# Dispatched rows of two expert stages read already turned, by transposing DMAs, in place of turns on TensorE

## The chip, the cores and the metric

The kernel runs on one core of one Trainium2 chip. The metric is the device time of one execution in microseconds (us); less is better. The time before is the median of three runs, 3177.68 us (3175.09 to 3180.09).

## The reference, cut to what matters

The input `x` is 16 x 256 = 4096 tokens of 256 features. Eight layers follow one another: four attention-like layers (`xattn`) and four feed-forward layers (`ffn`), each added to `x`. The change lies in two of the feed-forward layers, both mixtures of experts:

```python
# layer 0: each expert takes up to 512 tokens of each of the two choices
scores = softmax(xf @ router_w); weights, experts = top_k(scores, 2)
for k in range(2):
    xe = xf[tokens of expert e, at most 512]
    y  = gelu(xe @ w1[e]) @ w2[e]           # 256 -> 1024 -> 256
    out += y * weights[:, k]
...
# layer 1: no capacity; eight experts, two for each token, and one shared expert
g, u = x @ w_gate[e], x @ w_up[e]           # 256 -> 352
eo   = (silu(g) * u) @ w_down[e]            # 352 -> 256
```

## The kernel before

The kernel is written as stages, one after the other, each with its own queues for the five engines (`nc.Block`) and semaphores between them. Ahead of an expert stage a router decides the row of every token, and tokens are scattered by indirect DMAs into a table `rows` in memory, sorted by expert. A row of the table has 512 half-precision numbers: 256 high parts of a token's features and 256 low parts, so 1 KB. The value is kept as a sum of the two, and products are made of three terms (high x high, low x high, high x low).

`experts_stage` (line 1233) computes the experts. It is called four times; the argument `raw` (the table `rows`) is given in two of these calls, and only those are touched:

- **l0e** (line 2871): 8 experts, each with two blocks of 512 rows, so 16 blocks (`gt` = 4 tiles of 128 rows, `gn` = 512). The weights are loaded in single precision by SyncE's queue and split by ScalarE and VectorE (`convert`).
- **l1e** (line 2899): 39 blocks of 256 rows (`gt` = 2, `gn` = 256). The weights of a block come already split from `packed`, by one indirect DMA of GpSimd's queue for each block, 4 blocks ahead.

The work is a list `plan` of units. For each pair of blocks (`a` = 0 and 1) the units are: up of block 0, up of block 1, down of block 0, down of block 1. An up unit multiplies the weights (the matmul's stationary side) by the turned rows `xT` (features on the partitions, rows along the free side) into the PSUM tile `H`: 8 chunks of 6 matmuls of 512 columns in l0e, 3 chunks of 2 x 6 matmuls of 256 columns in l1e (line 1529). ScalarE applies the activation into `hf` (1586); VectorE multiplies by the gate in l1e (1619) and splits into `hh` (1625) and `hl` (1627). A down unit multiplies `hh` and `hl` by the second weights into `Y` (1544), 24 matmuls of 256 columns for a tile of 128 rows in l0e and 9 in l1e. VectorE copies `Y` to `y` (1635), and SyncE stores `y` to `results` (1400).

For a matmul the rows must be turned, with the features on the partitions. Before the change this takes three steps:

- SyncE loads a block as it lies into `rb` (line 1408), a ring of 4 (l0e) or 6 (l1e) buffers; it waits for `turned` before a buffer is taken again.
- TensorE turns it, in `turn(b)` (line 1486): for each half of 256 rows 8 transposes of 128 x 128 into the PSUM tile `T`. Blocks 0 and 1 are turned ahead of the first unit, and later ones after the second up unit of a pair and after its first down unit (`next_block`).
- ScalarE copies `T` to `xT` (line 1568), in `copy(b)`, one instruction for each half of 256 rows; `xT` has two buffers.

An up unit waits for `copied`. The order on each queue is written out by hand: SyncE's in l0e for expert n is the rows of block 2n, the weights of expert n, the rows of block 2n + 1, the stores of expert n - 1; in l1e six row loads at the start, then for each block its store and one row load. GpSimd copies an identity matrix at the start of both stages (line 1443).

Because `T` takes PSUM, `Y` has two banks with two tiles in each, and a tile of a down unit waits until VectorE has copied the tile two before it (`DEPTH` = 2).

## Time and profile before

| | |
|---|---|
| median of 3 runs | 3177.68 us (3175.09 to 3180.09) |
| span of the profiled execution, first to last instruction | 3092.9 us |
| what lies around the span (median less span) | 84.8 us |
| TensorE busy (matmuls) | 2527.4 us, 82% of the span |
| VectorE busy | 2162.5 us, 70% |
| ScalarE busy | 1301.5 us, 42% |
| GpSimd busy | 1035.7 us, 33% |
| DMA | 266.65 MB, mean 86 GB/s |
| l0e, first row load to last copy of a result | 494.5 to 854.8 us |
| l1e, first row load to last matmul of a down unit | 1155.3 to about 1415 us |

The profile is of one execution; of that execution the profile gives the span and no time of its own, so the median of the runs stands beside it. Times within it are counted from its first instruction. "PE" is TensorE, "PEld" its weight loads, "DVE" VectorE, "ACT" ScalarE, "POOL" GpSimd and "SPq" SyncE's queue. A matmul's duration in a row (some 270 ns for 256 columns) is that of one alone; they overlap, so what a series costs is read from the distance of the starts.

### The profile page before, as it was taken

The page shows a single profiled execution, that of the slowest core. Times are in us where ns is not written, and L with a number is a line of the kernel's source. Part 1 is how long each engine was busy: PE and PEld are TensorE (multiplying, and loading weights), DVE is VectorE, ACT ScalarE, POOL GpSimd, SP SyncE. Part 2 cuts the span into 40 slices and gives each one's busy share as a digit, 9 for nine tenths or more (in the row PEclk, how much of TensorE's full clock was granted, in tenths as well). Part 3 has the DMA queues.
Part 4 walks back from the last instruction along what each step waited for, and adds up shares of the span by engine and source line. Part 5 has one row for each costly group of instructions (what it writes and reads, how often), then busy time and mean ns, then how long its engine had stood idle before and what let it go on. Part 6 is the DMA issues. An engine that isn't in the chain of part 4 may idle for free. (4 is left out here: it accounts for less than half of the span.)

```text
span 3092.9 us, 57450 instructions
## 1 busy us (share of the span) xinstructions
PE 2527.4 (82%) x21340; PEld 1655.3 (54%) x21340; DVE 2162.5 (70%) x5536; ACT 1301.5 (42%) x2296; POOL 1035.7 (33%) x1446
## 2 busy tenths in 40 slices
PE   1989386999915599997999778885899999979973
PEld 0443264677614358995466544444565555656662
DVE  5898764665567766665678688977766555867757
ACT  1777443433312223332366646772322222356622
POOL 3452272110065361114466387861300000034330
PEclk9999588999957699998999888997999999979996
DMA  3331173332140247775611031100200000011001
GB/s 98 124 123 71 62 267 135 110 110 71 60 153 21 81 169 276 259 254 182 201 59 43 17 125 43 44 12 3 65 21 1 1 1 1 6 42 49 22 10 60
DMA packets 158280, 266.65 MB, mean 86 GB/s; under 512 B 23003, under 2 KB 106249, under 8 KB 151988
## 3 DMA queue, kind: packets, MB, share of 16 engines
q1 hardware_dynamic: 131316, 186.70, 18.1%
q0 software_dynamic: 17904, 76.23, 7.2%
q8 instruction: 172, 2.82, 0.4%
q10 hardware_dynamic: 8784, 0.04, 0.2%
q14 instruction: 104, 0.85, 0.1%
HBM read 174.99 MB, written 88.34 MB: 85 GB/s over the span
## 5 line engine op out<-in xcount | busy, mean ns | idle before, releaser
L1586 ACT ACTIVATE l2e_hf<-l2e_H 128x512 f32<-128x512 f32 x208 | 124.2, 597 | 381.9 <-PE l2e_H L1529 381.9
L1718 POOL TENSOR_TENSOR all_m_rstd<-all_m_sq,all_mhalf 128x8 f32<-128x8 f32 x24 | 39.6, 1649 | 558.4 <-DVE all_m_sq L1703 524.0
L788 DVE TENSOR_REDUCE l0a_mx<-l0a_S 128x2 f16<-128x512 f32 x256 | 167.8, 686 | 20.1 <-PE l0a_S L622 19.4
L1625 DVE CAST l2e_hh<-l2e_hf 128x512 f16<-128x512 f32 x208 | 92.8, 446 | 122.9 <-ACT l2e_hf L1586 108.6
L1529 PE MATMUL l0e_H<-l0e_xT,l0e_w 128*128 128x512 f16 x768 | 168.1, 381 | 0.0
L737 ACT ACTIVATE l0a_pf<-l0a_ST 128x512 f32<-128x512 f32 x256 | 146.6, 602 | 51.1 <-PE l0a_ST L636 50.9
L784 DVE CUSTOM_DVE_ANT_0 l2s_masked<-l2s_S,l2s_mq 128x128 f32<-128x128 f32 (+1 forms) x512 | 153.1, 349 | 19.5 <-PE l2s_S L622 19.3
L1529 PE MATMUL l2e_H<-l2o_hi,l2e_w 128*128 128x512 f16 x576 | 151.7, 382 | 15.8 <-DVE l2e_w L1601 15.8
L1529 PE MATMUL l1e_H<-l1e_xT,l1e_w 128*128 128x256 f16 (+1 forms) x1404 | 158.7, 275 | 2.8 <-DMA l1e_w<-packed,all_second_weight_row 2.8
L1529 PE MATMUL l2e_H<-l2e_hh,l2e_w 128*128 128x512 f16 x640 | 155.1, 379 | 0.0
L1627 DVE TENSOR_TENSOR l2e_hl<-l2e_hf,l2e_hh 128x512 f16<-128x512 f32 x208 | 147.2, 708 | 7.2
L1529 PEld LDWEIGHTS l1e_H<-l1e_xT,l1e_w 128*128 128x128 f16 (+1 forms) x1404 | 143.7, 107 | 15.3 <-DMA l1e_w<-packed,all_second_weight_row 3.1
L737 ACT ACTIVATE l2s_pf<-l2s_ST 128x384 f32<-128x384 f32 x256 | 119.3, 496 | 53.6 <-PE l2s_ST L636 53.1
L1586 ACT ACTIVATE l0e_hf<-l0e_H 128x512 f32<-128x512 f32 x128 | 76.4, 597 | 141.2 <-PE l0e_H L1529 141.2
L2689 POOL DMA_INDIRECT l1n_yb<-results,all_first_read x64 | 62.5, 977 | 196.0 <-POOLq L57 176.8
L1544 PE MATMUL l0e_Y<-l0e_w,l0e_hh 128*128 128x256 f16 x1024 | 124.7, 273 | 0.0
L1529 PEld LDWEIGHTS l0e_H<-l0e_xT,l0e_w 128*128 128x128 f16 x768 | 75.4, 98 | 89.7 <-issue 1.4
L788 DVE TENSOR_REDUCE l3a_mx<-l3a_S 128x2 f16<-128x512 f32 x128 | 88.2, 693 | 41.1 <-PE l3a_S L622 39.8
L581 POOL TENSOR_SCALAR_AFFINE_SELECT l2s_pf<-l2s_pf 128x256 f32<-128x256 f32 x256 | 100.9, 406 | 46.5 <-ACT l2s_pf L737 46.4
L1544 PE MATMUL l2e_Y<-l2e_w,l2e_hh 128*128 128x192 f16 x1024 | 109.5, 248 | 3.7 <-DVE all_x L1641 3.7
L788 DVE TENSOR_REDUCE l2a_mx<-l2a_S 128x2 f16<-128x512 f32 x128 | 87.5, 690 | 30.0 <-PE l2a_S L622 29.1
L1544 PEld LDWEIGHTS l0e_Y<-l0e_w,l0e_hh 128*128 128x128 f16 x1024 | 99.5, 98 | 11.6
(706 smaller groups left out, 7258.5 us busy)
## 6 DMA issues: line engine op xcount, KB each, us to landing
l0e_wf<-in_L_ffn_w SPq DMA_DIRECT2D x16, 1024.0 KB, 8.8
rows<-l0a_zeros SPq DMA_DIRECT2D x16, 640.0 KB, 5.9
l1e_rb<-rows SPq DMA_DIRECT2D x39, 256.0 KB, 9.0
results<-l1e_y SPq DMA_DIRECT2D x39, 256.0 KB, 2.2
l0a_kv<-in_ctx SPq DMA_DIRECT2D x16, 512.0 KB, 4.1
rows<-l0a_zeros SPq DMA_DIRECT2D x16, 512.0 KB, 4.9
l0d_p_cx<-in_ctx SPq DMA_DIRECT2D x16, 512.0 KB, 6.4
l0e_rb<-rows SPq DMA_DIRECT2D x16, 512.0 KB, 9.6
```

What stands on the lines that cost most here:

```text
L581: nc.gpsimd.affine_select(out=t, in_=t, compare_op=ALU.is_ge, fill=0.0, base=0, pattern=[[0, TB], [1, P]], channel_multiplier=-1).then_inc ...
L737: nc.scalar.activation(pf[n % NPF][:, 0:used], ST_ps[n % 2][:, 0:used], ACT.Exp).then_inc(probs, 1)
L784: m = nc.vector.tensor_tensor_reduce(masked[n % 2][u][:, 0:key_to[u]], ps[:, s_at[u]:s_at[u] + key_to[u]], mq[:, S - key_to[u]:S], 1.0, -3 ...
L788: m = nc.vector.tensor_reduce(mx[h % 2][:, :, i], ps[:, :].rearrange("p (u k) -> p u k", u=TB), AX.X, ALU.max)
L1529: mm = pe.matmul(bank[0:fn, :], W[par][0:kn, at + k * wd + f0:at + k * wd + f0 + fn], X, start=(done == 0), stop=(done == k_all - 1))
L1544: mm = pe.matmul(Y[u][:, 0:wd], X[0:kn, k, u * P:u * P + P], W[par][0:kn, at + k * wd:at + (k + 1) * wd], start=(done == 0), stop=(done == ...
L1586: nc.scalar.activation(hf[q % 4][0:fn, :], pair_of(q, lay)[0][0:fn, :], lay.func, scale=1.0 / WS).then_inc(acted, 1)
L1625: nc.vector.tensor_copy(high, v).then_inc(hi_done, 1)
L1627: nc.vector.tensor_tensor(low, v, high, ALU.subtract).then_inc(split, 1)
L1718: self.nc.gpsimd.tensor_tensor(out=(self.rstd, self.rstd2)[which][:, g], in0=(self.sq, self.sq2)[which][:, g], in1=self.g.mhalf[:, 0:self. ...
L2689: nc.gpsimd.indirect_dma_start(yb[n % NB][:, :], None, rows[:, :], bass.IndirectOffsetOnAxis(ap=to.read_row[n % 2][:, n // 2:n // 2 + 1], ...
```

## The change

The rows of a block are read by one DMA with a transpose (`dma_start_transpose`) straight from the table into `xT`, which now has the ring's depth (4 buffers in l0e, 6 in l1e). The tiles `rb`, `T` and `ident_h`, the functions `turn` and `copy`, the semaphores `turned` and `copied` and GpSimd's copy of the identity are gone. An up unit waits for `rows_in` of its block. SyncE waits with a buffer's next load for `upped` at the number of chunks that ends the up unit of the block that held it (`read_by`). `Y` has `gt` banks of its own, and a down tile waits for the copy of the tile `gt` before it.

```diff
--- before.py
+++ after.py
@@ -1242,13 +1242,12 @@
     tiles = 2 * gt * NPAIR if packed is None else gt
     NE = len(experts)
     STG = max(-(-a // P) * b for e in experts for a, b in e.mats)
-    HALVES, BLKS = gt // 2, NE * tiles // gt
+    BLKS = NE * tiles // gt
     RING = 4 if packed is None else 6
-    DEPTH = gt if raw is None else 2
     NW = min(2 if packed is None else 4, NE)
     cols = [max(e.cols for e in experts[i::NW]) for i in range(NW)]
 
-    plan, bank_of, bank_free, reads_of = [], [], [], {}
+    plan, bank_of, bank_free, reads_of, read_by = [], [], [], {}, []
     chunk = tile = bank = 0
     last_in = [None] * 4
     for first in range(0, NE, 1 if packed is None else 2):
@@ -1277,6 +1276,8 @@
                                 last_in[b] = chunk
                             chunk += 1
                         split_to[(l, a)] = chunk
+                        if l == 0:
+                            read_by.append(chunk)
                         if l:
                             reads_of[(a, (l - 1) % n_hbuf)] = ("upped", chunk)
                     else:
@@ -1316,17 +1317,10 @@
         hl = [[st.sb(f"hl{a}{i}", [P, FT, gn], F16) for i in range(n_hbuf)] for a in range(2)]
         hf = [st.sb(f"hf{i}", [P, gn]) for i in range(4)]
         H = st.ps("H", [P, 4, 512])
-        if raw is None:
-            Y = [st.ps(f"Y{i}") for i in range(gt)]
-        else:
-            pairs = [st.ps(f"Y{i}") for i in range(2)]
-            Y = [pairs[u % 2][:, u // 2 * D:(u // 2 + 1) * D] for u in range(gt)]
-            T = [st.ps(f"T{i}", [P, 2, KD, 2, P], F16) for i in range(2)]
-            rb = [st.sb(f"rb{i}", [P, gt, 2 * D], F16) for i in range(RING)]
-            xT = [st.sb(f"xT{i}", [P, 2, KD, gn], F16) for i in range(2)]
-            ident_h = st.sb("ident_h", [P, P], F16)
+        Y = [st.ps(f"Y{i}") for i in range(gt)]
+        if raw is not None:
+            xT = [st.sb(f"xT{i}", [P, 2, KD, gn], F16) for i in range(RING)]
             rows_in = [st.sem(f"rows_in{i}") for i in range(RING)]
-            ident_set, turned, copied = st.sem("ident_set"), st.sem("turned"), st.sem("copied")
 
         w_in = [st.sem(f"w_in{i}") for i in range(NSTG)]
         w_hi, w_lo = st.sem("w_hi"), st.sem("w_lo")
@@ -1404,10 +1398,9 @@
                     if raw is None or b >= BLKS:
                         return
                     if b >= RING:
-                        sp.wait_ge(turned, (b - RING + 1) * HALVES)
-                    sp.dma_start(rb[b % RING][:, :, :],
-                                 raw[b * gn:(b + 1) * gn, :].rearrange("(t p) d -> p t d", p=P)
-                                 ).then_inc(rows_in[b % RING], 16)
+                        sp.wait_ge(upped, read_by[b - RING])
+                    sp.dma_start_transpose(xT[b % RING][:, :, :, :].rearrange("p r k q -> p (r k) q"),
+                                           raw[b * gn:(b + 1) * gn, :]).then_inc(rows_in[b % RING], 16)
 
                 for n in range(NE):
                     if packed is None:
@@ -1439,8 +1432,6 @@
 
             @block.gpsimd
             def _(pool):
-                if raw is not None:
-                    nc.gpsimd.tensor_copy(ident_h[:, :], g.ident[:, :]).then_inc(ident_set, 1)
                 if pack is not None:
                     pack.fill(nc)
                 if send is not None:
@@ -1463,35 +1454,8 @@
                         w_all[n % NW][:, :], None, packed[:, :],
                         bass.IndirectOffsetOnAxis(ap=c[:, n:n + 1], axis=0)).then_inc(w_got[n % NW], 16)
 
-            def next_block(un):
-
-                if raw is None or (un.l, un.a) not in ((0, 1), (1, 0)):
-                    return BLKS
-                first = 2 * un.n if packed is None else un.n // 2 * 2
-                return first + (2 if un.l == 0 else 3)
-
             @block.tensor
             def _(pe):
-                def turn(b):
-                    if raw is None or b >= BLKS:
-                        return
-                    pe.wait_ge(rows_in[b % RING], (b // RING + 1) * 16)
-                    for j in range(HALVES):
-                        h = b * HALVES + j
-                        if h >= 2:
-                            pe.wait_ge(copied, h - 1)
-                        for r in range(2):
-                            for k in range(KD):
-                                for u in range(2):
-                                    m = pe.transpose(T[h % 2][:, r, k, u, :],
-                                                     rb[b % RING][:, 2 * j + u, r * D + k * P:r * D + (k + 1) * P],
-                                                     ident_h[:, :])
-                        m.then_inc(turned, 1)
-
-                if raw is not None:
-                    pe.wait_ge(ident_set, 1)
-                turn(0)
-                turn(1)
                 for un in plan:
                     ex, par, a = experts[un.n], un.n % NW, un.a
                     lay, m0 = layer_of(un), first_of_layer(ex, un.l)
@@ -1507,7 +1471,7 @@
                         col = (un.i * 2 + a) * gn if packed is None else 0
                         if raw is not None:
                             b = 2 * un.n + a if packed is None else un.n
-                            pe.wait_ge(copied, (b + 1) * HALVES)
+                            pe.wait_ge(rows_in[b % RING], (b // RING + 1) * 16)
                         for f, (f0, fn) in enumerate(lay.chunks):
                             q = un.at + f
                             before = bank_free[q]
@@ -1523,7 +1487,7 @@
                                         if un.l:
                                             X = (hh if x_hi else hl)[a][(un.l - 1) % n_hbuf][0:kn, k, :]
                                         elif raw is not None:
-                                            X = xT[a][:, 0 if x_hi else 1, k, :]
+                                            X = xT[b % RING][:, 0 if x_hi else 1, k, :]
                                         else:
                                             X = (hi if x_hi else lo)[:, k, col:col + gn]
                                         mm = pe.matmul(bank[0:fn, :],
@@ -1535,8 +1499,8 @@
                         at, wd = place(ex, m0), ex.mats[-1][1]
                         for u in range(gt):
                             t = un.at + u
-                            if t >= DEPTH:
-                                pe.wait_ge(added, t - DEPTH + 1)
+                            if t >= gt:
+                                pe.wait_ge(added, t - gt + 1)
                             k_all, done = 3 * len(lay.kt), 0
                             for W, x_hi in ((wh, True), (wh, False), (wl, True)):
                                 for k, (k0, kn) in enumerate(lay.kt):
@@ -1546,7 +1510,6 @@
                                                    start=(done == 0), stop=(done == k_all - 1))
                                     done += 1
                             mm.then_inc(downed, 1)
-                    turn(next_block(un))
 
             @block.scalar
             def _(act):
@@ -1559,20 +1522,8 @@
                                          wf[p.slot][0:p.rows, p.src:p.src + p.cols], ACT.Copy, scale=WS
                                          ).then_inc(w_hi, 1)
 
-                def copy(b):
-                    if raw is None or b >= BLKS:
-                        return
-                    for j in range(HALVES):
-                        h = b * HALVES + j
-                        act.wait_ge(turned, h + 1)
-                        nc.scalar.activation(xT[b % 2][:, :, :, j * 2 * P:(j + 1) * 2 * P],
-                                             T[h % 2][:, :, :, :, :].rearrange("p r k u q -> p r k (u q)"), ACT.Copy
-                                             ).then_inc(copied, 1)
-
-                copy(0)
                 for k in of_expert[0]:
                     convert(k)
-                copy(1)
                 if send is not None:
                     send.hi_parts(nc, act)
                 for un in plan:
@@ -1591,7 +1542,6 @@
                                 convert(later[t])
                         if pack is not None and un.a == 0:
                             pack.hi_part(act, un.i)
-                    copy(next_block(un))
 
             @block.vector
             def _(dve):
```

**TensorE in l1e, the first pair of blocks and the next.** `H` is the up units, `T` the turns, `Y` the down units. Before:

```order
L1529 MATMUL l1e_H<-l1e_xT,l1e_w 128x256 x24
L1529 MATMUL l1e_H<-l1e_xT,l1e_w 96x256 x12
L1529 MATMUL l1e_H<-l1e_xT,l1e_w 128x256 x24
L1529 MATMUL l1e_H<-l1e_xT,l1e_w 96x256 x12
L1486 MATMUL l1e_T<-l1e_ident_h,l1e_rb 128x128 x8
L1544 MATMUL l1e_Y<-l1e_w,l1e_hh 128x256 x3
L1544 MATMUL l1e_Y<-l1e_w,l1e_hl 128x256 x3
L1544 MATMUL l1e_Y<-l1e_w,l1e_hh 128x256 x6
L1544 MATMUL l1e_Y<-l1e_w,l1e_hl 128x256 x3
L1544 MATMUL l1e_Y<-l1e_w,l1e_hh 128x256 x3
L1486 MATMUL l1e_T<-l1e_ident_h,l1e_rb 128x128 x8
L1544 MATMUL l1e_Y<-l1e_w,l1e_hh 128x256 x3
```

With the change:

```order
L1493 MATMUL l1e_H<-l1e_xT,l1e_w 128x256 x24
L1493 MATMUL l1e_H<-l1e_xT,l1e_w 96x256 x12
L1493 MATMUL l1e_H<-l1e_xT,l1e_w 128x256 x24
L1493 MATMUL l1e_H<-l1e_xT,l1e_w 96x256 x12
L1508 MATMUL l1e_Y<-l1e_w,l1e_hh 128x256 x3
L1508 MATMUL l1e_Y<-l1e_w,l1e_hl 128x256 x3
L1508 MATMUL l1e_Y<-l1e_w,l1e_hh 128x256 x6
L1508 MATMUL l1e_Y<-l1e_w,l1e_hl 128x256 x3
L1508 MATMUL l1e_Y<-l1e_w,l1e_hh 128x256 x6
L1508 MATMUL l1e_Y<-l1e_w,l1e_hl 128x256 x3
```

The groups of 8 transposes between the up and the down units and between the two down units are gone; nothing else changes its place. In l0e it is the same with groups of 16.

**SyncE's queue in l0e, from expert 2 on.** `results` is the store, `wf` the weights; the brackets name the semaphore that is waited for. Before:

```order
L1408 DMA l0e_rb<-rows 128x4x512 [waits l0e_turned]
L1389 DMA l0e_wf<-in_L_ffn_w 128x2x1024 [waits l0e_w_lo]
L1389 DMA l0e_wf<-in_L_ffn_w 128x8x256 [waits l0e_w_lo]
L1408 DMA l0e_rb<-rows 128x4x512 [waits l0e_turned]
L1400 DMA results<-l0e_y 128x4x256 [waits l0e_added] x2
```

With the change:

```order
L1402 DMA_TRANSPOSE l0e_xT<-rows 128x4x512 [waits l0e_upped]
L1383 DMA l0e_wf<-in_L_ffn_w 128x2x1024 [waits l0e_w_lo]
L1383 DMA l0e_wf<-in_L_ffn_w 128x8x256 [waits l0e_w_lo]
L1402 DMA_TRANSPOSE l0e_xT<-rows 128x4x512 [waits l0e_upped]
L1394 DMA results<-l0e_y 128x4x256 [waits l0e_added] x2
```

The row loads keep their places in the queue and become transposes; their wait is for `upped` (TensorE's up unit) in place of `turned`.

## Rows read from the trace of the kernel before

**Rows 1.** the page: busy time of each engine, and the granted TensorE clock over 40 slices
```profile
PE 2527.4 (82%) x21340; PEld 1655.3 (54%) x21340; DVE 2162.5 (70%) x5536; ACT 1301.5 (42%) x2296; POOL 1035.7 (33%) x1446
...
PEclk9999588999957699998999888997999999979996
```

**Rows 2.** windows: a stretch of l0e and one of l1e (busy us, instructions, clock, DMA share, GB/s)
```profile
540.00:820.00 280.00, 280.00 (x2072) 193.66 (x2070) 174.47 (x307) 111.76 (x179) 21.05 (x29) 1.00 0.29 95
1180.00:1400.00 220.00, 220.00 (x2143) 202.22 (x2142) 146.24 (x382) 74.91 (x139) 30.92 (x33) 1.00 0.74 259
```

**Rows 3.** TensorE's waits in 505:856 (first row), its groups in 1155:1420 (the others)
```profile
PE l0e_T L1486 <- DMA l0e_rb<-rows: 5.2, 1, 5.2
...
L1529 PE MATMUL l1e_H<-l1e_xT,l1e_w 128*128 128x256 f16 (+1 forms) x1404 | 158.7, 275 | 2.8 <-DMA l1e_w<-packed,all_second_weight_row 2.8
L1544 PE MATMUL l1e_Y<-l1e_w,l1e_hh 128*128 128x256 f16 (+1 forms) x468 | 70.4, 272 | 1.7 <-DVE l1e_hl L1627 1.7
L1486 PE MATMUL l1e_T<-l1e_ident_h,l1e_rb 128*128 128x128 f16 x312 | 24.4, 224 | 6.9 <-DMA l1e_rb<-rows 6.9
```

**Rows 4.** tiles T of both stages: count, duration ns min/median/max, first and last start
```profile
L1486 PE MATMUL l0e_T<-l0e_ident_h,l0e_rb x256: 218/219/315, 498.4 to 802.0; 128*128 128x128 f16 x128
L1568 ACT ACTIVATE l0e_xT<-l0e_T x32: 1018/1021/1032, 499.5 to 802.7; 128x1024 f16<-128x1024 f16 x32
...
L1486 PE MATMUL l1e_T<-l1e_ident_h,l1e_rb x312: 217/219/315, 1158.9 to 1403.2; 128*128 128x128 f16 x156
```

**Rows 5.** timeline of TensorE in l0e: turns of one block (start us, us, engine ...)
```profile
615.88 1.06 PE L1486 MATMUL l0e_T<-l0e_ident_h,l0e_rb 128*128 128x128 f16 x16
616.77 1.04 PE L1544 MATMUL l0e_Y<-l0e_w,l0e_hh 128*128 128x256 f16 x8
```

**Rows 6.** timeline of l1e, one pair of blocks: TensorE and VectorE
```profile
1203.97 8.02 PE L1529 MATMUL l1e_H<-l1e_xT,l1e_w 128*128 128x256 f16 x72
...
1211.83 0.61 PE L1486 MATMUL l1e_T<-l1e_ident_h,l1e_rb 128*128 128x128 f16 x8
...
1212.28 0.49 PE L1544 MATMUL l1e_Y<-l1e_w,l1e_hh 128*128 128x256 f16 x3
...
1213.22 0.42 DVE L1627 TENSOR_TENSOR l1e_hl<-l1e_hf,l1e_hh 96x256 f16<-96x256 f32 x1
...
1213.56 0.41 DVE L1635 COPY l1e_y<-l1e_Y 128x256 f32<-128x256 f32 x1
...
1214.27 0.61 PE L1486 MATMUL l1e_T<-l1e_ident_h,l1e_rb 128*128 128x128 f16 x8
...
1214.71 0.49 PE L1544 MATMUL l1e_Y<-l1e_w,l1e_hh 128*128 128x256 f16 x3
...
1216.70 0.49 PE L1529 MATMUL l1e_H<-l1e_xT,l1e_w 128*128 128x256 f16 x3
```

**Rows 7.** timeline of the start of l0e
```profile
494.47 0.36 SPq L1408 DMA_DIRECT2D l0e_rb<-rows  x1
...
501.95 2.50 DVE L1601 SCALAR_TENSOR_TENSOR l0e_w<-l0e_wf,l0e_w 128x512 f16<-128x512 f32 x4 [29.45 <-ACT l0e_w L1558]
...
505.48 1.89 PE L1486 MATMUL l0e_T<-l0e_ident_h,l0e_rb 128*128 128x128 f16 x16 [5.19 <-DMA l0e_rb<-rows]
...
507.16 18.07 PE L1529 MATMUL l0e_H<-l0e_xT,l0e_w 128*128 128x512 f16 x78
```

**Rows 8.** DMA in 1180:1400 (queue: packets, MB, share of 16 engines; issue: KB, us to landing)
```profile
q0 software_dynamic: 5015, 38.78, 48.8%
q1 hardware_dynamic: 18485, 17.82, 24.8%
...
l1e_rb<-rows SPq DMA_DIRECT2D x32, 256.0 KB, 9.0
```

**Rows 9.** the page's queue of the smallest packets; SP's issue times of the l1e rows, ns
```profile
q10 hardware_dynamic: 8784, 0.04, 0.2%
...
L1408 SPq DMA_DIRECT2D l1e_rb<-rows x39: 371/473/1306, 1155.3 to 1380.9; - x39
```

## The prediction

> **What bounds the kernel now.** I read the page first. Over the span TensorE is the busiest engine with 82%, but that is an average over stages with different limits [rows 1]; what the change is worth must be read in the two stages that it touches. The second view is the windows of their steady parts [rows 2]. In 280 us of l0e and in 220 us of l1e TensorE's matmuls fill every microsecond, at a granted clock of 1.00 (2.4 GHz), while VectorE is busy 62% and 66%, ScalarE 40% and 34%. The third view is TensorE's waits [rows 3]: in the whole of l0e from 505 us on it waits once, 5.2 us at the start, for the rows of block 1; in l1e three times, for rows 6.9, for weights 2.8 and for a low half 1.7 us, all in the first pair of blocks. So TensorE's own time sets both stages, and what is taken from its queue comes off the span, as long as nothing else becomes later than TensorE. DMA engines are the next candidate: they are used 0.29 in l0e but 0.74 in l1e [rows 2].
>
> **What is removed.** There are 256 and 312 transposes [rows 4]. Their duration (218 ns) is not their price, since they overlap; the price is the distance from the first of a group to the next instruction. In l0e the 16 of a block take 616.77 - 615.88 = 0.89 us [rows 5]; in l1e the 8 of a block 1212.28 - 1211.83 = 0.45 and 1214.71 - 1214.27 = 0.44 us [rows 6].
>
> - l0e, blocks 2 to 15: 14 x 0.89 = 12.5 us off the path.
> - l1e, blocks 2 to 38: 37 x 0.445 = 16.5 us off the path. Blocks 0 and 1 are turned while TensorE waits for the first weights anyway [rows 3], so they give nothing.
> - Start of l0e: the first up unit begins at 507.16, behind the turns of block 1, which begin at 505.48, when its rows land. The first weight matrix is split at 501.95 + 2.50 = 504.45 [rows 7]. With the change the unit needs only that and block 0, whose transfer is issued at 494.47, 10 us earlier; block 1 is not needed until the unit after it. The gain is at most 507.16 - 504.45 = 2.7 us, and nothing if block 0's slower transfer holds up the weights behind it. I take 2.
> - ScalarE's copies (32 of 1.02 us in l0e, 39 in l1e) [rows 4] lie beside TensorE's work, which never waits for them. They give nothing. GpSimd's copy of the identity, 0.3 us, lets the first weight gather of l1e start earlier, but six transposes stand beside it: nothing. The two more banks of Y in l0e remove a wait that TensorE does not show; in l1e the depth stays 2.
>
> **What is late next.** In l1e the down unit of block 1 of a pair needs the last low half of its up unit, and its first tile needs the copy of the first tile of the unit before (depth 2). Before, the last up matmul is followed by 0.45 of turns, 1.99 of the first down unit and 0.44 of turns. The low half is done at 1213.22 + 0.42 = 1213.64 and the copy, which VectorE takes right behind it, at 1213.56 + 0.41 = 1213.97; TensorE comes at 1214.71 [rows 6]. Without the turns it comes at 1211.83 + 1.99 = 1213.82, ahead of the copy. VectorE's chain hangs on the up unit's end and does not move. So there is a new wait of 0.15 us, and about 0.1 to 0.2 more for the release and for filling the pipeline again, which is not shown before; I take 0.3, from 0 to 0.6. Over 19 pairs that gives back 5.7 us (0 to 11.4). In l0e the first down unit of a pair is 10.5 us long (four tiles of 24 matmuls), so nothing of this arises there.
>
> **What is added: 16 transposes of 512 KB and 39 of 256 KB.** No row shows one. First the time at which they are asked for: SyncE's new wait is for the up unit of the block 4 or 6 earlier, which stands behind a store that waited for that block or a later one, so it never decides, and the stores behind it are not held. A block of l1e is read about five blocks (30 us) ahead of its use, a landing now takes 9.0 us [rows 8], so what matters is throughput, not latency.
>
> The price of throughput: in l1e the DMA engines work 0.74 x 220 us; a pair takes 1216.70 - 1203.97 = 12.73 us [rows 6], a block 6.37, so 4.71 us of DMA for each block. The hardware queue has 24.8% of 220 us = 54.6 us for 34.5 blocks, half rows and half stores (both 256 packets of 1 KB): 0.79 us for the 256 rows, and 3.92 us for all the rest [rows 8]. The new period by TensorE is 6.37 - 0.445 + 0.15 = 6.07 us. **TensorE stays the bound if a transpose of 256 rows costs at most 6.07 - 3.92 = 2.15 us of DMA, 2.7 times the plain transfer.** In l0e there is far more room (0.29 of 21.7 us).
>
> The bounds. Below: 0.79 us, the plain transfer; a quicker one would gain nothing, as TensorE does not wait for these transfers past the start. Above: two adjoining numbers of a row go to two partitions. If each became a packet of its own, at the 0.2% x 16 x 3092.9 / 8784 = 11 ns of the page's smallest packets [rows 9], a block would cost 131072 x 11 ns / 16 = 90 us, and the kernel over 3 ms more. In between, the nearest row is the landing of the same rows, 9.0 us, were one transpose to hold its queue that long. I take under 2.15 us, since the same number of bytes and the same kind of queue are nearest to the plain row; this is my least certain choice. Issuing takes SyncE 0.37 to 1.3 us for the plain load [rows 9], one instruction for each block as before; it has 6 us for each.
>
> By the rows, a 128 x 128 turn on TensorE is worth 0.056 us of its time. The Trainium skill ("VectorE: DVE Perf Modes", The three transpose paths) gives 1309 ns for one through the DMA crossbar; eight of them one after another would be an estimate of 10.5 us for a block of l1e. The same skill ("Advanced Engine Details and Errata", X-Bar Transpose (TRN2)) holds that transposing DMAs are as fast as ordinary ones, which would leave the sum as it stands. No row of before can decide between them.
>
> **The sum.** 12.5 + 2 + 16.5 - 5.7 = 25.3 us less. The span was 3092.9, so 3067.6; the median of the runs is 84.8 above the span, which I leave as it is: 3177.7 - 25.3 = **3152 us**, 0.8% faster. Its own range, by the start (0 to 2.7) and the new wait (0 to 11.4): 3144 to 3160.
>
> **The rivals.**
>
> 1. Transposes that don't fit beside l1e's other traffic (the other side). Place: the DMA engines or SyncE's queue in l1e. Mechanism: a transposing transfer costs several times its bytes, or they run one at a time. From 2.15 us for a block it shows; from 2.45 l1e loses what it gained; from about 2.8 (2.45 + 14.5 / 39), 3.6 times the plain price, the kernel is slower. Priced by the landing row, 9.0 us for each block: (9.0 - 6.37) x 39 = 103 more in l1e, 14.5 less in l0e, where 21.7 us still hold it: 3266 us. For it: l1e's engines have only a quarter to spare, small packets cost far more for a byte, and the turned layout is made of small pieces. Against it: l0e hides anything up to some 16 us, and a queue with 30 us of lead evens out bursts. Chance 0.35. By the skill's 1309 ns for a tile, 10.5 us, it would be (10.5 - 6.37) x 39 - 14.5, or 3324.
> 2. Half of it: transposes of about 3 times the plain price. l1e is where it was, l0e keeps its 14.5: 3163, between 3160 and 3180. Chance 0.17.
> 3. The new wait is not there, because VectorE's chain moves with TensorE's, or a release is quicker: 3146. It lies within the forecast's own range and has no chance of its own.
>
> **How the numbers follow.** Forecast 0.48, rival 1 0.35, rival 2 0.17. A measurement of this kernel can tell about 0.2%, 6.4 us, from no change, so "same" is 3171 to 3184. Faster: 0.48 and 0.11 of rival 2, 0.59; same: the other 0.06 of it; slower: 0.35. The range begins at 3142, just under the forecast's own. To leave no more than 2 in 10 out it must reach through rival 2 and half of rival 1, to 3270.
>
> **What would show it.** Right: no L1486 rows; in the windows a pair of l1e at about 12.1 us and an expert of l0e at 41.7 in place of 43.5; TensorE still without waits in l0e and, in l1e, 19 waits of 0.2 to 0.4 us for VectorE's copy or low half; the first up unit of l0e at about 505. The transposes' landing within 20 us, and the DMA share of l1e under 0.9. Wrong: waits of TensorE for DMA into xT or w in l1e (rival 1 or 2, by their sum), SyncE's issues of several microseconds, or stores that land so late that VectorE waits for `stored`.

## The result, and the profile after

The changed kernel takes 3198.22 us (median of 20 runs, 3179.18 to 3235.61), the kernel before beside it 3180.03 us (20 runs, 3173.57 to 3185.43). The ratio is **1.0068 [1.0049, 1.0088]: slower by 0.7%**, where 0.8% faster was forecast. The range of 3142 to 3270 holds it, but only because it was drawn wide enough for the rivals; the forecast's own 3144 to 3160 misses it. The ratios here and below are of the fast runs alone, which leaves out any run more than 1.5% above the fastest of its kernel (here one of the 20). The spread is news too: 56 us from the fastest to the slowest run, against 12 for the kernel before.

The windows of the kernel after, in the order l0e (the stretch of [rows 2]), then l1e, its columns as in [rows 2]:

```profile
540.00:820.00 280.00, 280.00 (x1911) 186.74 (x1909) 185.40 (x327) 91.78 (x160) 20.29 (x28) 1.00 0.37 94
...
1260.00:1280.00 20.00, 19.86 (x182) 18.03 (x181) 14.29 (x38) 4.58 (x12) 2.42 (x3) 1.00 1.13 235
1280.00:1320.00 40.00, 30.07 (x245) 25.63 (x244) 18.45 (x50) 4.58 (x12) 4.68 (x5) 0.87 1.04 206
1320.00:1360.00 40.00, 39.58 (x359) 35.50 (x357) 26.98 (x71) 7.64 (x20) 6.55 (x7) 1.00 1.07 270
```

l0e is as clean as before, and l1e is not: in one stretch of 40 us TensorE is busy 30, its clock is 0.87, and the DMA engines, though over 1.0 busy, move 206 GB/s where the next stretch moves 270.

**l0e** went nearly as forecast. The answer to [rows 7] and [rows 3], from the timeline of its start (TensorE), and the last down units from the tile's listing (count, duration, first and last start):

```profile
504.20 8.17 PE L1493 MATMUL l0e_H<-l0e_xT,l0e_w 128*128 128x512 f16 x26 [24.59 <-DVE l0e_w L1551]
```

```profile
L1508 PE MATMUL l0e_Y<-l0e_w,l0e_hh x1024: 272/273/273, 527.3 to 839.9; 128*128 128x256 f16 x171
```

In the trace of before the same listing ends at 854.1, 14.2 us later, where 14.5 were forecast. But 1.3 of these are an earlier begin of the whole stage in this execution: its first row load is issued at 493.18, that of before at 494.47. From this load to the last down matmul l0e takes 359.6 us before and 346.7 after, so 12.9 us were won (13.6 in e1, 13.5 in e13). The turns' 12.5 are there: an expert takes 631.63 - 589.95 = 41.68 us, 43.46 before. The start gave 0.4 here (1.1 in e1): the first up unit begins 1.7 us sooner after the first load, but 1.3 are lost again in its first matmuls. They now run while the granted clock is still 0.50 (windows 504:506 and 506:508; 1.00 from 510 on), a time that before was mostly spent on the turns. TensorE waits for nothing else in the stage.

**l1e** took 1501.2 - 1229.4 = 271.8 us from its first up to its last down matmul; before it was 1414.9 - 1163.6 = 251.3. The answer to [rows 6], a pair of blocks where nothing disturbs it (timeline, TensorE):

```profile
1259.17 8.02 PE L1493 MATMUL l1e_H<-l1e_xT,l1e_w 128*128 128x256 f16 x72
1267.03 0.49 PE L1508 MATMUL l1e_Y<-l1e_w,l1e_hh 128*128 128x256 f16 x3
...
1268.69 1.12 PE L1508 MATMUL l1e_Y<-l1e_w,l1e_hh 128*128 128x256 f16 x6
...
1269.98 0.82 PE L1508 MATMUL l1e_Y<-l1e_w,l1e_hh 128*128 128x256 f16 x6
...
1271.31 4.86 PE L1493 MATMUL l1e_H<-l1e_xT,l1e_w 128*128 128x256 f16 x43
```

A pair takes 1271.31 - 1259.17 = 12.14 us; 12.1 was forecast. The new wait is in it too: the six matmuls across the border of the down units take 1.12 where six others take 0.82, so 0.30. If all pairs were like this one, the forecast would have held. (TensorE's matmuls show no wait here; its weight loads do, 17 times, 8.3 us in all, for VectorE's low half `hl` and not for its copy.) The losses stand in the chain of waits of l1e (engine, what waits, for what: us, times, longest):

```profile
DVE l1e_y L1585 <- DMA results<-l1e_y: 36.2, 13, 15.0
...
PE l1e_H L1493 <- DMA l1e_xT<-rows: 13.8, 1, 13.8
...
PE l1e_H L1493 <- DMA l1e_w<-packed,all_second_weight_row: 12.6, 2, 11.0
...
PE l1e_H L1493 <- DVE l1e_hf L1569: 7.3, 1, 7.3
...
PE l1e_Y L1508 <- DVE l1e_y L1585: 2.7, 2, 1.8
```

The first wait for weights (11.0) is the stage's start and is nothing new: from the last matmul of l1s to the first up matmul pass 11.3 us, before 11.9. New are 13.8 us for the rows of block 1, then 7.3 + 2.7 + 1.6 for things that hang on VectorE and on a late gather, and the lower clock behind such pauses. VectorE in turn waits 36 us for its stores. Why the stores are late is seen in SyncE's queue (timeline; the duration is that of issuing), the answer to [rows 9]:

```profile
1221.69 29.68 SPq L1402 DMA_TRANSPOSE l1e_xT<-rows  x6
...
1273.43 17.04 SPq L1402 DMA_TRANSPOSE l1e_xT<-rows  x1
1290.52 3.45 SPq L1394 DMA_DIRECT2D results<-l1e_y  x1
...
1307.10 1.27 SPq L1402 DMA_TRANSPOSE l1e_xT<-rows  x1
...
1309.13 5.21 SPq L1402 DMA_TRANSPOSE l1e_xT<-rows  x1
```

Merely to issue a transpose holds SyncE 1.3 us at best, 5.2 in the second of two that follow one another within 2.3 us, and here 17.04. The store behind that one leaves at 1290.52. VectorE gets its buffer back at 1297.44 and TensorE, behind it, resumes at 1298.67:

```profile
1297.44 0.76 DVE L1585 COPY l1e_y<-l1e_Y 128x256 f32<-128x256 f32 x2 [15.03 <-DMA results<-l1e_y]
```

The plain loads of before took 0.47 us in the median [rows 9]. The answer to [rows 8], in a stretch without a jam (a jam is a time in which the DMA engines are busy, move little and TensorE pauses; 1306 to 1366; queue: packets, MB, share of 16 engines; q1 is SyncE's, q0 the weight gathers):

```profile
q0 software_dynamic: 1438, 11.13, 54.6%
q1 hardware_dynamic: 12813, 5.13, 49.0%
```

Packets are now of 256 bytes for the rows, 1024 for a block where there were 256.

Two facts about the times are needed below. Chips differ: the kernel before takes about 3178 us beside e1 to e4 and 3094 beside e5 to e15, so times are compared only with before of the same chip, as a ratio or a difference. And most of the difference is one stage that the change doesn't touch, l1s, which takes 170.6 us from its first to its last matmul in the kernel after and 103.0 in the profile of before. The kernel after, l1s, TensorE's waits:

```profile
PE l1s_Y L1508 <- issue: 58.5, 23, 12.9
```

e1 to e4 show 56 to 59 us of it, e5 to e15 none. The changed kernel shows it in e1 and not in e13, so the change does not bring it. The profile of before, like that of e8, has none, which is most of its 84.8 us between span and median. The expected times of e5 to e7 were still written for a kernel before of 3178 us; they are read as differences to it.

### The profile page after: what moved, and what is told of

The parts are those of the page before. It is cut to its first block and busy times, and to the rows that moved or that the text cites. A ratio compares the mean times of both kernels' runs of the same rounds, so it can differ in the third digit from the quotient of the medians.

```text
span 3184.9 us, 56187 instructions
## 1 busy us (share of the span) xinstructions
PE 2507.9 (79%) x20772; PEld 1618.7 (51%) x20772; DVE 2160.3 (68%) x5536; ACT 1231.4 (39%) x2225; POOL 1028.7 (32%) x1444
## 5 line engine op out<-in xcount | busy, mean ns | idle before, releaser
L1493 PE MATMUL l1e_H<-l1e_xT,l1e_w 128*128 128x256 f16 (+1 forms) x1404 | 163.4, 279 | 33.7 <-DMA l1e_xT<-rows 13.8
L1493 PE MATMUL l2e_H<-l2o_hi,l2e_w 128*128 128x512 f16 x576 | 151.5, 381 | 15.8 <-DVE l2e_w L1551 15.8
L1537 ACT ACTIVATE l1e_hf<-l1e_H 128x256 f32<-128x256 f32 (+1 forms) x117 | 44.7, 382 | 240.4 <-PE l1e_H L1493 200.6
L1453 POOL DMA_INDIRECT l1e_w<-packed,all_second_weight_row x39 | 36.6, 939 | 308.0 <-PE l1e_Y L1508 220.5
```

Of the source, the lines that this page charges most:

```text
L1453: nc.gpsimd.indirect_dma_start(w_all[n % NW][:, :], None, packed[:, :], bass.IndirectOffsetOnAxis(ap=c[:, n:n + 1], axis=0)).then_inc(w_go ...
L1493: mm = pe.matmul(bank[0:fn, :], W[par][0:kn, at + k * wd + f0:at + k * wd + f0 + fn], X, start=(done == 0), stop=(done == k_all - 1))
L1537: nc.scalar.activation(hf[q % 4][0:fn, :], pair_of(q, lay)[0][0:fn, :], lay.func, scale=1.0 / WS).then_inc(acted, 1)
```

## The experiments

In a name, l0 and l1 are the stages l0e and l1e.

**e1_again: the changed kernel, unaltered.**

> The changed kernel unchanged, for a second profile. Theory A (the transposes of l1e overload the DMA engines: a 256-byte packet of a transpose takes about 35 ns against 12 for as many bytes of a plain one): 3185 to 3215 us; l1e again with DMA share about 1.0 and waits of TensorE for xT, for weights and for stores in bursts; the stage l1s between the two transposing stages, where the first profile shows TensorE stuttering with 'issue' for 43 us, shows no stutter, as nothing is transposed there. Theory B (transposes disturb the fetching of instructions in later stages): the 43 us of 'issue' in l1s come again.

Measured: 3194.21 us against 3178.39, ratio 1.0063 [1.0047, 1.0080]; l1e 266.5 us, with the same waits (rows 13.5, weights 13.1, `hf` 5.2) and 32.9 us for the first six issues. The loss repeats, and so do the issue waits of l1s.

**e2_l0_only and e3_l1_only: the change in one stage alone.** The code of both ways, chosen by a flag:

```diff
-                  bias=..., raw=rows)
+                  bias=..., raw=rows, xbar=True)      # e2: call of l0e; e3: call of l1e
```

> Only l0e reads its rows by transposing DMAs; l1e turns on TensorE as before. Theory A: 14.2 us less than before (12.5 of turns, 1.7 of start), 3163 to 3168, runs close together as before. Theory B: the gain is eaten in l1s or elsewhere, 3178 or more, with a wide spread.

> Only l1e reads its rows by transposing DMAs. Theory A: before + 18 + 14 = about 3212 (3200 to 3230), with the wide spread of the changed kernel; l1s without 'issue'. Theory B, where the damage is done by l0e's transposes to stages behind them: at most 3180.

Measured: e2 3168.58 us, 0.9970 [0.9958, 0.9982], 9.8 us won; l1e stays at 250.7 us. Of the 12.9 us by which l0e is shorter in e2's trace too, 9.8 reach the medians; where the rest goes isn't shown. e3 3224.00 us, 1.0135 [1.0116, 1.0155], 45.6 us lost; l1e takes 298 us. So l0e gains most of what was forecast, and all of the loss is l1e's. e3's waits:

```profile
DVE l1e_y L1650 <- DMA results<-l1e_y: 67.6, 11, 17.6
...
PE l1e_H L1544 <- DVE l1e_hf L1634: 20.3, 3, 9.5
...
PE l1e_H L1544 <- DMA l1e_w<-packed,all_second_weight_row: 16.3, 2, 10.2
```

**e4_plain: the same bytes by plain DMAs.**

```diff
-sp.dma_start_transpose(xT[b % RING]..., raw[b * gn:(b + 1) * gn, :])
+sp.dma_start(xT[b % RING]..., raw[b * gn:(b + 1) * gn, :].rearrange("(t p) d -> p t d", p=P))
```

> The changed kernel with plain DMAs of the same bytes (1 KB packets) in place of the transposes; the rows are not turned, so the two expert stages compute with data in the wrong places, at the same shapes. It shows what the turns on TensorE alone are worth. Both theories: 3150 to 3156, as in my sum (14.2 in l0e, 10 to 14 in l1e), pairs of l1e of 12.1 us without hiccups, spread as narrow as before. If it is not faster than before, the loss has nothing to do with transposing.

Measured: 3155.55 us, 0.9925 [0.9913, 0.9938], 22.8 us won, where the forecast's sum was 25.3. l1e takes 239.5 us, 11.8 less than before (forecast 16.5 - 5.7 = 10.8). TensorE's waits in it are two, for the first weights and the first low half:

```profile
PE l1e_H L1495 <- DMA l1e_w<-packed,all_second_weight_row: 12.3, 1, 12.3
PE l1e_Y L1510 <- DVE l1e_hl L1579: 1.7, 1, 1.7
```

Its window 1300:1360 and SyncE's row loads in it (count, issue ns min/median/max):

```profile
1300.00:1360.00 60.00, 59.29 (x536) 53.11 (x534) 41.58 (x110) 11.45 (x30) 9.37 (x10) 1.00 0.78 271
```

```profile
L1402 SPq DMA_DIRECT2D l1e_xT<-rows x39: 370/472/1864, 1223.8 to 1439.2; - x39
```

So the terms on TensorE and VectorE hold, as a sum, to 2.5 us. What fails is what the transposing transfers do, and nothing else in the change.

**e5_pieces: plain DMAs in packets of 256 bytes.**

```diff
+for t in range(gt):
+    sp.dma_start(xT[b % RING][:, :, :, t * P:(t + 1) * P]...,
+                 raw[b * gn + t * P:...].rearrange("p (j q) -> p j q", q=P)).then_inc(rows_in[b % RING], 16)
```

> The changed kernel with plain DMAs that move the same bytes in as many packets as the transposes have (256 bytes each; one DMA for each 128 rows, so 2 and 4 for a block), rows not turned, so data in the wrong places. In the steady part of l1e the transposes cost 34 ns a packet, 2.2 us a block, against 48 ns for 1 KB. Theory A1 (it is the small packets): as slow a packet here, 30 to 35 ns, DMA share of l1e about 1.0, the time as the changed kernel's, about 3195. Theory A2 (it is the turning itself, which needs more than a small plain packet): a plain packet of 256 bytes takes 15 to 20 ns, share 0.8 to 0.85, time 3152 to 3160, as with plain packets of 1 KB.

Measured: 3073.56 us against 3093.87, 0.9934 [0.9921, 0.9948]; l1e 243.5 us, with a wait for rows of 3.2. Its queues in 1230:1290:

```profile
q0 software_dynamic: 1440, 11.14, 52.5%
q1 hardware_dynamic: 13205, 5.17, 32.2%
```

As many packets as in the kernel after, but q1 uses 32.2% and not 49.0%, and nothing jams. (These DMAs are two for a block, the transposes one.) So behind the start it is not the small packets but the turning that costs.

At the start the size of the packets does count. There are the queues of the kernel after in 1231:1246, while TensorE waits for the rows of block 1, and those of e5 in 1153:1159:

```profile
q0 software_dynamic: 346, 2.72, 67.6%
q1 hardware_dynamic: 837, 0.21, 33.9%
```

```profile
q0 software_dynamic: 304, 2.37, 95.7%
q1 hardware_dynamic: 305, 0.08, 5.7%
```

Beside the gathers (q0) the rows barely move in either, 14 and 13 GB/s. In e5 the two queues get as many packets each, and one of the rows' is 256 bytes; with packets of 1 KB (e4, 1234:1240) 308 beside 285 carry 48 GB/s. But in e5 the gathers run at 395 GB/s and are soon done, so TensorE waits 3.2 us for the rows; beside transposes they run at 181. When they are done in the kernel after, the rows move at 223 GB/s (1249:1252).

**e6_l0_twice and e7_l1_twice: each transpose a second time, into a spare buffer.**

```diff
+if twice:
+    sp.dma_start_transpose(spare[b % RING]..., raw[b * gn:(b + 1) * gn, :]).then_inc(spare_in[b % RING], 16)
```

> Only l0e transposes, and each of its 16 transposes is issued a second time, into a buffer that nobody reads. Theory A: l0e has room, with one transpose of 512 KB at 4.4 us of DMA and 4.7 of all the rest in 20.8 us a second one is hidden: the time of e2, 3165 to 3175 (weights land 4 us later but are split 10 us after landing). Rival: what counts is SyncE's time (2.3 to 8.5 us an issue) or the order behind it: then TensorE waits for weights at each expert, 3180 or more.

> Both stages transpose, and each of l1e's 39 transposes is issued a second time into a spare buffer. Theory A (DMA engines are full): a block of l1e then takes 3.9 + 2 x 2.2 = 8.3 us at the least against 6.07, so 39 x 2.2 = 87 us and more on the changed kernel: 3280 to 3330. Rival (hiccups come from order and start only, with time to spare on the engines): under 3230.

Measured: e6 3084.13 us, 0.9967 [0.9955, 0.9979], which is e2's ratio: in l0e even the second transpose is hidden, except at the start, where the first up unit comes 14.8 us behind the first load in place of e2's 11.1. e7 has four runs, 3161, 3167, 3236 and 3249 us, so 68 to 155 more than before (median 108), where 102 to 152 were expected by the theory of full engines and under 52 by its rival: neither holds as it stands. In its trace (of the 3167) l1e takes 336 us, 56 more than e13's, the DMA share 1.11 over 1180:1480 at 222 GB/s. The dose counts in l1e (the edit also makes SyncE wait for the spare buffer's load before) and not in l0e, where in 540:820 the share with two transposes is 0.48.

**e8_before_again: the kernel before, unaltered.**

> The kernel before, unchanged, for a second profile. Its first profile has a span 85 us under the time of its runs and no 'issue' waits of TensorE in l1s, while all five later profiles have about 57 us of them there, whatever is transposed, and spans within 15 us of their runs. If these waits belong to every execution and the first profile was the exception, this one shows them too, with a span of about 3165 to 3185; if they come from the changes, they are absent again.

Measured: 3095.71 us, span 3094.0, no issue waits in l1s. With e13 this says that they go with the chip, or the time at which it was used, and not with the change; it cleared most of the 84.8 us.

**e9_act_stores: l1e's stores go out from ScalarE's queue.**

```diff
+if packed is not None:
+    act.wait_ge(added, un.at + gt)
+    act.dma_start(rows_out[...], y[un.a][:, :, :]).then_inc(stored[un.a], 16)
```

> The changed kernel, but l1e's 39 stores are issued from ScalarE's queue, so that they no longer stand behind transposes whose issue takes up to 17 us on SyncE's queue. In the changed kernel VectorE waits 36 us in l1e for stores, and TensorE 7 to 10 us behind it. Theory A2 (DMA engines are full, 1.04 in the steady part, so every hiccup stays): the time stays near 1.006 of before, 1.002 at best. Theory C (the order in SyncE's queue makes the hiccups; the engines would keep up): 10 to 15 us less than the changed kernel, 1.001 to 1.003 of before.

Measured: 3084.77 us (3079.43 to 3086.04) against 3093.51, 0.9967 [0.9954, 0.9980]. TensorE's waits in l1e, all at its start:

```profile
PE l1e_H L1495 <- DMA l1e_w<-packed,all_second_weight_row: 10.4, 1, 10.4
...
PE l1e_H L1495 <- DMA l1e_xT<-rows: 9.9, 1, 9.9
...
PE l1e_Y L1510 <- DVE l1e_hl L1583: 1.7, 1, 1.7
```

Its window 1240:1300, and the queues in it (q1 now has transposes alone, q10 the stores):

```profile
1240.00:1300.00 60.00, 59.30 (x537) 53.08 (x535) 42.16 (x110) 11.48 (x30) 8.67 (x11) 1.00 1.00 274
```

```profile
q1 hardware_dynamic: 10560, 2.62, 33.5%
q10 hardware_dynamic: 2720, 2.62, 12.9%
```

The DMA share is 1.00 and TensorE runs as fast as in e4. "The engines are full" is therefore not what costs time. VectorE no longer waits for stores, the later pauses are gone, and the spread of the runs shrinks from 22 us (e13) to 7. Against the changed kernel 26 us were won (below), where 10 to 15 were expected. Two things changed, though. The stores no longer stand behind transposes; and the transposes no longer stand behind stores, so they leave 3.9 and 8.2 us apart, where the kernel after has 2.3 and 9.8, and issuing one is quick: 1.33 us in the median, and none over 2.1 once the first six are out (17.04 in the kernel after). So it is shown that stores and transposes in one queue cost the time behind the start. How much of it is stores that are held, and how much the transposes' own long issues, no run separates.

**e10_gate and e11_both: block 1's rows ahead of the third weight gather**; e11 has e9's stores as well.

```diff
+if n == 2:
+    pool.wait_ge(rows_in[1], 16)
```

> The changed kernel, but GpSimd issues l1e's third weight gather only when block 1's rows have landed. At the start of l1e six transposes and four gathers of 1.1 MB compete, and TensorE waits 13.8 us for block 1's rows. A transpose takes 5.2 us of SyncE's queue beside a gather and 1.3 us alone. If gathers slow the transposes, the 13.8 us fall to under 3 and the time by about 10 us: 1.003 of before. If the transposes are as slow by themselves, nothing is won.

> Both of the last two edits. If both are right: 0.997 to 1.000 of before, with l1e at about 245 us; still not the 0.9925 of plain packets, since the DMA engines are full.

Measured: e10 3110.26 us, 1.0050 [1.0027, 1.0073]; e11 3112.94, 1.0053 [1.0022, 1.0085]. The wait for rows fell from 13.8 to 5.7 us in e10, as meant, but weights then cost TensorE 24.5 us in four waits, and the time is that of the changed kernel (e13). e11 was expected at 0.997 to 1.000 with l1e at 245 us; l1e took 278, so the gate turned e9's 0.9967 into 1.0053. In e11, with the stores out of SyncE's queue, the windows of the start and of the time behind it are:

```profile
1180.00:1200.00 20.00, 11.44 (x76) 8.81 (x75) 4.32 (x12) 1.15 (x3) 1.07 (x2) 0.68 1.20 160
1200.00:1240.00 40.00, 29.80 (x225) 24.84 (x224) 17.04 (x46) 4.25 (x12) 4.41 (x5) 0.83 1.19 179
...
1300.00:1380.00 80.00, 79.16 (x716) 71.12 (x715) 55.82 (x147) 15.66 (x41) 12.07 (x13) 1.00 0.96 278
```

The engines are 1.2 busy and move 160 GB/s; 100 us later they move 278 at 0.96. Queue order is not all: there is a jam in the DMA itself. Stores in a queue of their own are late in it too (VectorE waits 30.8 us for them), and so are gathers (23.0 us of TensorE's waits, the 11.3 at the stage's start among them); TensorE's clock falls with such pauses (0.68).

**e12_mix: in l1e only the odd blocks come turned, the even ones as before.** l0e as in the change.

```diff
+dma_turned = lambda b: xbar or (half and b % 2 == 1)
```

> l0e transposes by DMA, in l1e only the odd blocks do, the even ones are turned on TensorE as before. Theory A2: DMA share of l1e in between, about 0.9, so no hiccups; TensorE is rid of 19 turns of 0.445 us, 8.5 us, on top of what l0e gives (0.997): 0.994 to 0.996 of before, the best of all correct kernels. Rival: even so a transpose beside a gather blocks SyncE's queue at times, and stores come late: 0.998 or more.

Measured: 3076.62 us (3070.97 to 3081.69), 0.9949 [0.9935, 0.9962], faster than both kernels, as expected. l1e 243.2 us, VectorE's waits for stores 3.5 us, no pause behind the start.

**e13_after_here, e14_flight, e15_mix_act: on one chip.** e13 is the changed kernel; e14 lets at most two transposes of l1e be in flight; e15 is e12 with e9's stores.

```diff
+if packed is not None and b >= 2:                      # e14
+    sp.wait_ge(rows_in[(b - 2) % RING], ((b - 2) // RING + 1) * 16)
```

> The changed kernel, unaltered, beside the two that follow, so that all are read against the same runs of before. On a chip where before takes 3094 us and shows no issue waits in l1s, every theory has before's time less 14.5 (l0e) plus what l1e loses, 15 to 21 us by the two traces of it so far: 3094 to 3101 us, ratio 1.000 to 1.002. If l1e's loss here is under 8 us, the loss itself depended on the chip; if the ratio stays at 1.006, something beside l1e is lost.

> The changed kernel, but in l1e SyncE starts a block's transpose only when the one two blocks ahead has landed, so at most two are in flight. If the jams come from several transposes that pile up (six at the start, and those that follow a pause) and SyncE's issues of 10 to 17 us are its queue's descriptors being full, no issue is over 6 us, TensorE's hiccups for hf, y and w behind the start go, and the time is 3070 to 3080 us. If the hold is a single transpose that meets a weight gather, issues of over 10 us stay, and with them the stores behind; time as that of the changed kernel or up to 10 us more, since SyncE now also waits.

> The mixed kernel (l0e turned by DMA; in l1e odd blocks by DMA and even ones on TensorE) with l1e's stores issued from ScalarE's queue. If what the transposes still cost the mixed kernel is stores held behind them in SyncE's queue, some of its waits at the start go and it takes 3070 to 3075 us. If at half the number no store is held (VectorE waited 3.5 us for stores there, TensorE not at all behind the start), it stays within 3 us of 3076.6, or gets up to 5 us slower by ScalarE's issues and waits ahead of its activations.

Measured, against 3094.29 of before: e13 3111.22 us, 1.0069 [1.0046, 1.0091], the ratio of the first measurement again, though l1s is quiet here; l1e 280.6 us. The expected ratio was too low because it took l1e's loss from the two traces at hand, whose executions (3186.7 and 3182.5 us) lay under the medians of their runs. Against e13, e9's stores won 26 us by the differences to before (16.9 more, 8.7 less).

e14 3110.09 us (3090.64 to 3144.46), 1.0053 [1.0021, 1.0086]. Its SyncE queue (of its longest execution, 3144 us):

```profile
1176.11 10.09 SPq L1404 DMA_TRANSPOSE l1e_xT<-rows  x1
...
1186.93 18.17 SPq L1404 DMA_TRANSPOSE l1e_xT<-rows  x1
```

Issues of 10 and 18 us with no more than two transposes in flight, and a median as e13's: the number of them that pile up is not what makes a jam. The first branch of the expectation fell.

e15 **3073.83 us (3070.28 to 3077.38), 0.9935 [0.9922, 0.9948]**, the best version. Its l1e in 1200:1380, and its transposes' issues (ns) and landings; then the same of e12:

```profile
1200.00:1380.00 180.00, 180.00 (x1699) 164.73 (x1698) 122.93 (x321) 47.74 (x102) 27.17 (x29) 1.00 0.81 262
```

```profile
L1418 SPq DMA_TRANSPOSE l1e_xR<-rows x19: 1232/1233/7282, 1142.8 to 1345.5; - x19
...
DMA to landing us min/median/max: 3.3/3.3/6.8
```

```profile
1200.00:1380.00 180.00, 180.00 (x1703) 164.96 (x1701) 124.12 (x324) 48.42 (x104) 26.23 (x28) 1.00 0.97 263
```

```profile
L1418 SPq DMA_TRANSPOSE l1e_xR<-rows x19: 1569/5284/6953, 1140.7 to 1348.3; - x19
...
DMA to landing us min/median/max: 6.7/10.8/15.0
```

The same transposes beside the same traffic: 1.2 us to issue and 3.3 to land when the stores use another queue, 5.3 and 10.8 when they share it, and the DMA share is 0.81 against 0.97. TensorE is full in both, so the times lie within 3 us (the intervals overlap): with half the transposes, moving the stores is not shown to win anything.

## Why the prediction was wrong

**Right.** The bound was TensorE in both stages. The turns' price: l0e is 12.9 to 13.6 us shorter (14.5 forecast), e2 won 9.8 of it in the medians. The start of l0e gave 0.4 us, since 1.3 of its 1.7 went to a low clock (1.1 in e1; 0 to 2.7, taken 2). The new wait of l1e is 0.30 us for a pair, as taken. e4, where the transfers are plain, gave 22.8 of the sum's 25.3 us. That ScalarE's copies gave nothing by themselves was not tested apart; e4 leaves no room for a gain from them.

**The price of throughput** ("I take under 2.15 us") was close. From the queue in 1306:1366, with stores at 47 ns for a 1 KB packet (24.8% x 3520 us / 18485, [rows 8]), (49.0% x 960 us - 2560 x 0.047) / 10250 packets = 34 ns for each transposed packet, and for a block of 1024 packets on 16 engines 2.2 us. In e9 it is 33.5% x 960 / 10560 = 30 ns, 1.95 us a block. That is 2.5 to 2.8 times the plain 0.79, just about the prediction's threshold of 2.7, and TensorE is 99% busy in both windows. By this step alone the time would have been near the forecast, or rival 2's. These are means. By the trace's packet records of 1306:1366 a transposed packet took 18 ns in the median, just as e5's plain ones, and one in a hundred over 450: the mean is made by a few packets that stand still. Nor is the mean a constant: over 1200:1340 it is 20 ns in e15 and 49 in e12, where the stores share the queue. The 1309 ns for a tile that the Trainium skill gives ("VectorE: DVE Perf Modes", The three transpose paths) is not what a stream costs here, since eight tiles take 2 us of the engines. The Trainium skill's "TRN2 transpose DMAs are as fast as regular DMAs" ("Advanced Engine Details and Errata", X-Bar Transpose (TRN2)) fits the median here and not the mean: e5's plain packets of the same size cost (32.2% x 960 - 120) / 10650 = 18 ns.

**The steps that failed.** Two stand in the prediction's part on what is added. "So it never decides, and the stores behind it are not held": I looked only at SyncE's semaphore wait, and the instruction itself holds the queue. "Issuing takes SyncE 0.37 to 1.3 us for the plain load [...]; it has 6 us for each": the plain row was carried over to another kind of DMA, whose issue takes 1.2 to 18.3 us. Nearly each store of l1e stands behind one. Once a transposing issue lasts longer than VectorE's two `y` buffers can bridge, the store, VectorE's copy and TensorE follow in turn; the trace shows this chain at 1273.43 to 1298.67. e9 takes stores and transposes apart: the later pauses vanish, and slower by 0.7% becomes faster by 0.3%. Not shown is whether short issues alone, with the stores where they were, would have done the same.

A third step, as dear as these two, is "what matters is throughput, not latency". True of a steady state, it is false at the stage's start, where TensorE waits 13.8 us for the rows of block 1, and e9 still 9.9. The price of either is read by cutting l1e at its first down matmul (us):

| | first up to first down matmul | first to last down matmul |
|---|---|---|
| before | 10.5 | 240.9 |
| e4, plain packets of 1 KB | 9.2 | 230.5 |
| e5, plain packets of 256 bytes | 13.1 | 230.5 |
| the changed kernel (after, e1, e13) | 25.5, 27.2, 26.6 | 246.3, 239.3, 254.1 |
| e9 | 23.7 | 230.5 |
| e12, e15 | 10.5, 10.2 | 232.8, 232.8 |

Against plain packets the changed kernel loses 16 to 18 us at the start, the waits and the lower clock behind them, and 9 to 24 behind it. e9 wins back all of the second and almost nothing of the first, which is why its l1e (254 us) stays 14 us behind e4's. Some 4 us of the first go with the small packets (e5). e12 and e15 lose nothing at the start.

**The rivals.** Rival 1 had the side and, in "SyncE's queue in l1e", the place, but its mechanism, a steady period above TensorE's, is not what happened: in stretches without a jam the mean price was 1.95 to 2.2 us a block, under its 2.8. Hence its 88 us more, where 18 were measured. It also charged l0e's block, of 512 rows, with the 9.0 us of 256; at 18, beside the stage's 4.7 us of other DMA, the 21.7 us would not have held it.

**Open.** What starts a jam, in which the engines are 1.04 to 1.2 busy over 20 to 40 us and move 160 to 206 GB/s in place of 270. Not small packets (e5), not the number of transposes in flight (e14), not a full share as such (e9 ran at 1.00 without one), and not the stores' queue alone (e11's start). That the gathers run at half their rate beside transposes at the start (181 GB/s, 395 in e5) belongs to it. It was seen only with transposes and weight gathers together, and a gather moved later brought more of it (e10, e11); whether their meeting is the cause was argued and not isolated. Why e3, with l0e unchanged, loses 45.6 us and not 25.6 (e1's 15.8 and e2's 9.8) is open as well; its loss lies behind the start of l1e, 273.5 us there.

## What to carry to other kernels

When a DMA is exchanged for another kind, price three things: its time on the engines, its landing, and how long issuing it holds its queue, and then name who stands behind it there. A transposing DMA pays where the engines are mostly idle (l0e: 0.29 to 0.37, gain kept even at double the number); in the stage at 0.74 turning only half of the blocks by DMA won (e12), and with all of them turned by DMA the results' stores had to leave the queue that issues them (e9). Look at the start of a stage by itself, where everything is asked for at once and nothing has a lead. A mean over a steady window hides pauses: read the waits of the whole stage and the spread of the runs beside it.

## What the runs showed of the hardware

- Issuing a DMA that transposes 256 rows of 1 KB held SyncE's queue 1.23 us at least. When stores shared the queue the median was 2.6 (after), 3.4 (e13) and 5.3 (e12), with stores in another queue 1.33 (e9) and 1.23 (e15); the longest took 18.3 (e3, e11). A plain one took 0.37 to 1.9 (e4), a plain one of 128 rows in packets of 256 bytes 0.5 to 8.7 (e5).
- A transposed packet of 256 bytes cost 30 to 34 ns of an engine in l1e in the mean (after, e9; 20 in e15, 49 in e12) and 18 in the median, a plain one of 256 bytes 18 in both (e5), one of 1 KB 47.
- Beside gathers at the start of l1e, rows in packets of 256 bytes moved at 13 to 14 GB/s, transposed or plain, and in packets of 1 KB at 48; in e5 and e4 both queues got about as many packets (305 and 304, 308 and 285).
- With stores in a queue of their own and half the number (e15) transposes landed in 3.3 us.
- The share of the DMA engines is no measure of their work when transposes run: e11 shows 1.20 at 160 GB/s and 0.96 at 278, e12 and e15 0.97 and 0.81 at 263 and 262.
- After pauses of TensorE its granted clock fell to 0.68 (e11) and 0.87 (after) in the mean of a window, between its levels of 1.2 and 2.4 GHz (0.5 and 1.00), and was 1.00 where it stayed busy.
- The changed kernel lost 58 us on one chip (e1), in TensorE's issue waits of l1s, and nothing on another (e13).
